# A six-layer transformer on one core: the next layer's projection weights split in halves, at places spread over two cycles

## The reference, cut to what matters

```python
def attn_layer(x, Wqkv, qs, ksc, Wo):
    qkv = x @ Wqkv
    ...
    q = l2norm(q) * qs
    k = l2norm(k) * ksc
    q = q * cos * scale + rotate_half(q) * sin * scale
    k = k * cos * inv + rotate_half(k) * sin * inv
    out = local_attention(q, k, v)
    return out @ Wo
for i in range(DEPTH):
    x = attn_layer(shift_tokens(x), Wqkv[i], q_scale[i], k_scale[i], Wo[i]) + x
    x = ffn_layer(shift_tokens(x), ln_g[i], ln_b[i], W1[i], b1[i], W2[i], b2[i]) + x
```

## Time and profile before

| | |
|---|---|
| median of 3 runs | 3810.37 us (3803.43 to 3812.31) |
| the profiled execution | 3809.82 us, its span 3808.0 us |
| TensorE, VectorE, ScalarE, GpSimd busy | 92%, 78%, 71%, 63% of the span |
| mean granted clock of TensorE | 0.978 |
| first projection of the layers | at 686.59 us of the span |

### The profile page before, as it was taken

One profiled execution on the slowest core, in us unless ns is written; L12 is line 12 of the kernel. 1 busy time (PEld: TensorE's weight loads), 2 busy tenths in 40 slices (PEclk: granted clock), 3 DMA queues, 4 the chain that ended last, 5 costly groups with the idle time before them and its releaser, 6 DMA issues. The chain is left out here.

```text
span 3808.0 us, 161553 instructions
## 1 busy us (share of the span) xinstructions
PE 3516.9 (92%) x67234; PEld 2893.7 (76%) x67234; DVE 2986.5 (78%) x4277; ACT 2686.3 (71%) x4153; POOL 2393.2 (63%) x2866
## 2 busy tenths in 40 slices
PE   5888888599999999999999999999999999999995
PEld 3555555378888888888888888888888888888874
DVE  3455554588888888888888888888888888888874
ACT  2444444377777778877778877888778887887772
POOL 1010000577777777777777777777777777777762
PEclk9999999799999999999999999999999999999997
DMA  1000000132222332222322223222232222322221
GB/s 54 4 3 3 6 3 3 41 89 69 67 70 63 74 90 70 70 66 73 90 66 66 66 72 90 66 66 66 72 89 67 67 71 63 75 71 68 67 66 56
DMA packets 161761, 228.28 MB, mean 60 GB/s; under 512 B 42259, under 2 KB 60633, under 8 KB 161497
## 3 DMA queue, kind: packets, MB, share of 16 engines
q1 hardware_dynamic: 161624, 226.85, 23.8%
HBM read 21.00 MB, written 4.19 MB: 7 GB/s over the span
## 5 line engine op out<-in xcount | busy, mean ns | idle before, releaser
L1109 POOL TENSOR_TENSOR by_cos<-by_cos,by_sin 128x1024 f32<-128x1024 f32 x384 | 921.3, 2399 | 49.2 <-DVE by_sin L1453 49.2
L1115 POOL TENSOR_TENSOR by_cos<-by_cos,norms 128x1024 f32<-128x1024 f32 x384 | 724.0, 1907 | 0.5 <-issue 0.3
L1451 DVE TENSOR_TENSOR by_cos<-proj,turns 128x1024 f32<-128x1024 f32 x384 | 470.0, 1224 | 216.6 <-ACT squares L1344 216.2
L1188 PE MATMUL proj<-qkv_hi,xs_hib 128*128 128x512 f32 x1152 | 523.9, 455 | 57.8 <-DVE by_sin L1453 42.2
L1344 ACT ACTIVATE squares<-proj 128x1024 f32<-128x1024 f32 x384 | 392.5, 1022 | 179.9 <-PE proj L1190 172.6
L1324 ACT ACTIVATE vb<-proj 128x1024 f32<-128x1024 f32 x192 | 195.4, 1017 | 422.7 <-PE proj L1190 401.1
L1453 DVE TENSOR_TENSOR by_sin<-proj,turns 128x1024 f32<-128x1024 f32 x384 | 466.1, 1214 | 0.0
L1457 DVE TENSOR_REDUCE sumsb<-squares 128x16 f32<-128x1024 f32 x384 | 464.0, 1208 | 1.5 <-DVE w_lo L1514 1.5
L1190 PE MATMUL proj<-qkv_hi,xs_lob 128*128 128x512 f32 x1152 | 459.2, 399 | 0.8 <-issue 0.8
L1189 PE MATMUL proj<-qkv_lo,xs_hib 128*128 128x512 f32 x1152 | 458.5, 398 | 0.0
L1197 PE MATMUL ring<-ident,by_cos 128*128 128x128 f32 x3072 | 404.4, 275 | 1.7 <-POOL by_cos L1115 0.8
(11 more groups left out here) (172 smaller groups left out, 8208.7 us busy)
## 6 DMA issues: line engine op xcount, KB each, us to landing
v_win<-vb SPq DMA_DIRECT2D x1152, 128.0 KB, 2.4
v_win<-vb SPq DMA_DIRECT2D x768, 64.0 KB, 2.0
in_qkv<-L_ffn_Wqkv SPq DMA_DIRECT2D x12, 768.0 KB
wo<-L_ffn_Wo SPq DMA_DIRECT2D x6, 512.0 KB, 4.0
x_tok<-L_attn_x SPq DMA_DIRECT2D x8, 256.0 KB, 4.7
residual<-x_tok SPq DMA_DIRECT2D x8, 256.0 KB, 2.0
o_x<-residual SPq DMA_DIRECT2D x1, 2048.0 KB, 7.9
out<-o_x SPq DMA_DIRECT2D x8, 256.0 KB, 2.3
```

Source lines behind the costliest of these rows:

```text
L1109: nc.gpsimd.tensor_tensor(both, both, by_sin[:, j, :], ALU.add).then_inc(e[f"{w_}_added"].sem, 1)
L1115: nc.gpsimd.tensor_tensor(heads, heads, inverse, ALU.mult).then_inc(e[f"{w_}_ready"].sem, 1)
L1188: nc.tensor.matmul(out, xs_hi[:, tile], qkv_hi[:, cols], start=True, stop=False)
L1451: nc.vector.tensor_tensor(of_heads(by_cos[:, t % 2, j, :]), heads, table(0), ALU.mult)
```

## The change

The three conversions of 1024 columns become six of 512, and each has a place of its own: a table, NEXT_WEIGHTS, says before which step of cycle 14 (-2) or 15 (-1) of a layer's end it is put. ScalarE rounds all six halves. VectorE subtracts four (lo_q0, lo_q1, lo_k1, lo_v0), GpSimd two (lo_k0, lo_v1). The four tables of turns are issued one by one. All semaphores are per half, and the readers wait for both halves of what they use: GpSimd's first XSd of the new layer for q, the first Cq for k and for the turns, the first Ck for v. At the start of the stage each engine does its own pieces first, in the order of the table.

```diff
+NEXT_WEIGHTS = {
+    "Act": {(-2, "MK:1"): "hi_q0", (-2, "EXP:0"): "hi_q1", (-2, "GEL"): "hi_k1", (-1, "EV:1"): "hi_k0",
+          (-1, "EXP:-1"): "hi_v0", (-1, "EX:-1"): "hi_v1"},
+    "DVE": {(-2, "AM"): "lo_q0", (-2, "Rk:3"): "turn_0 turn_1", (-2, "XN"): "lo_q1 turn_3",
+          (-1, "R:-2"): "turn_2", (-1, "Cq:2"): "lo_k1 lo_v0"},
+    "Pool": {(-1, "N:1"): "lo_k0", (-1, "Aq:2"): "lo_v1"},
+}
...
-    if at == -LEAD and engine in ("Act", "DVE"):
-        steps += [(("NQ", k), 0, "", 0) for k in range(3)]
+    if at == -LEAD:
+        steps += [((piece,), None, "", 0) for piece in " ".join(NEXT_WEIGHTS.get(engine, {}).values()).split()]
...
+        if end is None and at is not None and at >= STEPS - HALVES:
+            pieces = NEXT_WEIGHTS.get(engine, {}).get((at - STEPS, token), "").split()
+            steps += [((piece,), None, "", 1) for piece in pieces]
...
-        if tile == PER * STEPS - 1 and end is None:
-            for k, (act, dve) in enumerate((("Qq", "Rq"), ("Qk", "Rk"), ("EV", ""))):
-                if (engine, name) in (("Act", act), ("DVE", dve)):
-                    steps.append((("NQ", k), 0, "", 1))
-            if (engine, name) == ("DVE", "Rk"):
-                steps.append((("NT",), 0, "", 1))
-        if (engine, name) == ("DVE", "Cq") and tile == PER * STEPS and end is None:
-            steps.append((("NQ", 2), 0, "", 1))
...
+        def columns_of(x):
+
+            at = PART[x[0]] * INNER + int(x[1]) * (INNER // 2)
+            return slice(at, at + INNER // 2)
...
-                        pool.wait_ge(p_lo, new * 3 + 1)
+                        for half in "01":
+                            pool.wait_ge(p_lo["q" + half], new + 1)
...
+                elif kind[:3] == "lo_":
+                    x = kind[3:]
+                    cols = columns_of(x)
+                    pool.wait_ge(p_hi[x], new + 1)
+                    nc.gpsimd.tensor_tensor(qkv_lo[:, cols], in_qkv[:, cols], qkv_hi[:, cols].bitcast(F32),
+                                            ALU.subtract).then_inc(p_lo[x], 1)
...
+                elif kind[:3] == "hi_":
+                    x = kind[3:]
+                    act.wait_ge(loaded, all_loaded(new))
+                    if when[1] >= 0:
+                        event, tile = f"{x[0]}_proj", PER * STEPS - 1 - PER * p
+                        wait_tile(act, event, tile, when)
+                    cols = columns_of(x)
+                    copy(qkv_hi[:, cols], in_qkv[:, cols]).then_inc(p_hi[x], 1)
...
-                        dve.wait_ge(p_turns, new + 1)
+                        dve.wait_ge(p_turns, new * 4 + 4)
+                        for half in "01":
+                            dve.wait_ge(p_lo[("k" if w_ == "q" else "v") + half], new + 1)
...
+                elif kind[:5] == "turn_":
+                    n = int(kind[5:])
+                    scale = in_qs if n < 2 else in_ks
+                    nc.vector.scalar_tensor_tensor(
+                        out=turns[:, n, :, :], in0=tables[:, n, :, :], scalar=(QK_SCALE if n < 2 else 1.0) / ROOT_SCALE,
+                        in1=scale[:, :].unsqueeze(1).broadcast_to([P, TILES, DH]), op0=ALU.mult, op1=ALU.mult)\
+                        .then_inc(p_turns, 1)
```

More of the change, by code:

```diff
@@ L961, in layers_stage @@
         pool_ready = sem("pool_ready")
-        p_hi, p_lo, wo_loaded, p_w2 = sem("p_hi"), sem("p_lo"), sem("wo_loaded"), sem("p_w2")
+        wo_loaded, p_w2 = sem("wo_loaded"), sem("p_w2")
+        p_hi, p_lo = ({x: sem(f"p_{part}_{x}") for x in ("q0", "q1", "k0", "k1", "v0", "v1")} for part in ("hi", "lo"))
         p_w1_hi, p_col, p_used = sem("p_w1_hi"), sem("p_col"), sem("p_used")
@@ L1495, in step @@
                         .then_inc(e["x_mid"].sem, 1)
[L1496 to L1499, removed]
+                elif kind[:3] == "lo_":
+                    x = kind[3:]
+                    cols = columns_of(x)
+                    dve.wait_ge(p_hi[x], new + 1)
                     nc.vector.tensor_tensor(qkv_lo[:, cols], in_qkv[:, cols], qkv_hi[:, cols].bitcast(F32),
[L1501 to L1505, removed]
+                                            ALU.subtract).then_inc(p_lo[x], 1)
+                elif kind[:5] == "turn_":
[5 more added lines that the diff above has]
+                        .then_inc(p_turns, 1)
                 elif kind == "NF":
@@ L1520, in step @@
                     ffn(kind, b, when)
[L1522 to L1528, removed]
             def ffn(kind, b, when):
```

## The result

The changed kernel takes 3819.15 us (median of 8 runs, 3815.22 to 3824.95), the kernel before beside it 3807.82 (8 runs, 3803.43 to 3812.31): the ratio is 1.003, with a 95% interval of 1.0019 to 1.0041. The profiled execution took 3824.72 us, its span is 3822.9. One execution of the kernel before, among those beside e5_v_whole and b3_balanced, took 6572.57 us at a mean clock of 0.56 and enters no number here.

The account below looks back on a forecast made before the run. TensorE was busy 92% of the span, and a layer boundary cost 4.02 us more than two plain cycles. Boundaries +7.1, stage start +1.2 and clock +1 made +9.3 on 3809.8: 3819 us, range 3803 to 3828.

Parts of the forecast that it names:

- base: The profiled execution of the kernel before, 3809.8 us, 0.6 below the median of three runs, to which the terms were added.
- start term: At the stage's start, GpSimd's pieces ahead of its first XSd delay the first projection: +1.2 us once, bounds 0.3 and 2.5.
- clock term: TensorE stands still longer at each boundary, so the granted clock falls more: +1 us in all, bounds -1 and +4.
- Exclusion: VectorE operations reading two SBUF tensors and GpSimd ones wait out each other's whole instruction; whichever has waited goes next.
- The cost of a boundary: Cycles 14 and 15 at a layer's end: 5.4 us over two plain cycles instead of 4.0, five times +1.4 = +7.1.
- Splitting gained 0.7 us at XN: Cycle 14, VectorE: with the split, XN starts at t 29.43 against 30.17, winning 0.7 us there.
- the pair: Cycle 15, VectorE: lo_k1 waits for GpSimd's Ak:1 to 35.94, lo_v0 follows, Cq:2 starts at 37.14 instead of 35.08.
- Rival (a): Cycle 15: GpSimd's lo_v1 goes ahead of lo_v0, so lo_v0 and Cq wait 1.2 us more; 3825; chance 0.20.
- the 0.1 us: Cycle 15: lo_v1 is ready at about 36.64, lo_v0 starts at 36.54; Ak:1 that much later would let lo_v1 first.
- Rival (d): The clock drops at every boundary: the forecast + 4, 3823 us; chance 0.10.

Follow-up runs that it names:

- e5_v_whole: e4_halves_old_places with VectorE's two halves of v made one operation of 1024 columns again; 3814.17 us, ratio 1.0001 to the kernel before.
- b3_balanced: Changed kernel with Ak:1 ahead of N:1, VectorE's and GpSimd's pieces re-placed, all lo pieces on VectorE at the stage's start; 3802.65 us, 0.9970 of the kernel before.
- e1_read_psum: Changed kernel with VectorE's lo pieces at layer ends reading one PSUM input times zero instead of two SBUF tensors; 3804.43 us, ratio 0.9990 to the kernel before.
- e3_ak_first: Changed kernel with GpSimd's Ak:1 ahead of N:1 and turn_2 moved to cycle 14; 3811.98 us, ratio 1.0005 to the kernel before.
- e6_hi_v1_early: Changed kernel with ScalarE's hi_v1 moved directly behind hi_v0; 3829.58 us, ratio 1.0048 to the kernel before.
- the second profile: Changed kernel run and profiled again without any edit; 3822.29 us, ratio 1.0031 to the kernel before.
- e2_no_gpsimd_pieces: Changed kernel with GpSimd's two pieces at layer ends only raising their semaphores; 3812.26 us, ratio 1.0007 to the kernel before.
- e4_halves_old_places: Changed kernel with the six halves at the places of the old whole pieces, none on GpSimd; 3829.38 us, ratio 1.0045 to the kernel before.

## Why the prediction was right, point by point

The time was forecast at 3819.0 and came out at 3819.15. Part of that is luck: the kernel before had 3807.8 in the 8 runs beside the changed one, 2.6 below the three runs on which the forecast was put, and the sum was 2 us short (9.3 forecast, 11.3 measured): a base too high, a start term too large and a clock term too small nearly cancel. By its steps:

- **Exclusion, its length and, at the layers' ends, who goes next** held. lo_q0 at t 22.57, ending 24.74 (22.58 and 24.77 forecast); XN at 29.42 (29.43); Ak:1 at 33.68 (33.69); Cq:2 at 37.12 (37.14); Pk at 39.52 (39.55). e1_read_psum showed that the SBUF read is the cause, e3_ak_first that it is this one operation of GpSimd. That of two the one that has waited goes next, which the prediction gave as a rule, did not hold at the start of the stage in three of the kernels (b3_balanced above).
- **The cost of a boundary** was forecast at 67.2 and is 67.23 with the clock at 1.00. Splitting gained 0.7 us at XN, as said, and lost more at the pair.
- **Rival (a)** was put at 1.2 us a boundary above the forecast. e6_hi_v1_early, in which it happens, has Cq:2 1.07 us later than the changed kernel (t 38.19 against 37.12) and 1.4 us more in a boundary, where the clock fell in both: 69.7 in the mean against 68.3 at the nine such ends of the changed kernel. It needed the 0.1 us, and lo_v1 missed them: it was ready at 2719.30, and Cq:2 shows that lo_v0 had begun at about 2719.2 (2719.78 less the 0.60 of a half).
- **The start of the stage** was put at +1.2. At the first projection it is +0.9 (6.63 against 5.70), +1.3 in the second profile. By the first XC nothing of it is left: 105.5 and 107.0 against 106.75. The step that failed is that a later first projection makes a later stage; over the ten profiles the way from the first score to the first XC is 105.5 to 107.3 us, with no relation to where the first projection lies. That the delay comes from GpSimd's pieces is not shown either, as b3_balanced had +1.2 without them.
- **The clock** was put at +1, with bounds of -1 and +4. Worked out from the boundary pairs, the changed kernel lost 341.89 - 5 x 67.23 = 5.7 us to it, and 3.7 in the second profile, against 330.15 - 5 x 65.82 = 1.05 before: +2.7 to +4.7. This is the mis-sized term. I took one drop in five to stay the usual case, though the forecast itself had TensorE stand longer than before at every boundary. Rival (d), each boundary slowed, which had a chance of 0.10, is what happened, with the start term gone and so without its 3823. The step should have taken 1.05 x 5 from the earlier trace rows, as the rival did, or most of it.

So the sum by its terms is +7.1 (boundaries), 0 (start), +2.7 to +4.7 (clock): +9.8 to +11.8, and 11.3 was measured, 12.1 the second time.

**What stays open** is what decides the clock. The changed kernel and e6, with waits of 2.33 and 3.40 us ahead of Pk, lost it at 14 of 15 ends. The kernel before and e5_v_whole wait 2.02 and 2.09 us ahead of V and lost it at one in five each, as did e3_ak_first with 1.85 us there and e2_no_gpsimd_pieces with 1.51 ahead of V and 1.36 ahead of Pk. b3_balanced, with nothing above 0.95 us in these cycles, lost it at none. That far the length of the wait would do. But e1_read_psum has nothing above 1.28 us there and lost it at three ends, and e4_halves_old_places, with two waits at each (2.09 us ahead of V, 1.95 us for GpSimd's f_rstdb 13 us later), at all five. No run here separates the length of a wait from where it lies.

## What to carry to other kernels

Before a VectorE operation on two SBUF tensors is moved or split, lay it over GpSimd's timeline: its price is what is left of the GpSimd instruction that it meets, here up to 2.2 us on a half of 0.69, and a step of GpSimd moved by one place (and a turn with it) was worth 1.7 us a boundary where the split was worth 0.7. Splitting an operation also opens a place in its midst, into which an instruction that has waited can go; split only where nothing waits. And a wait of TensorE that a change makes longer should be charged with the matmuls behind it at half speed as well. Here a wait of 2.33 us had that price nine times in ten, 1.05 us in the mean; waits of 1.85 to 2.09 us had it at one end in five.

## What the runs showed of the hardware that was not expected

- Two halves back to back on VectorE let a waiting GpSimd instruction in between them: 3.48 us for a pair that is 1.21 as one piece. But not always: at the start of the stage, xs_lo on GpSimd had to sit out VectorE's next two pieces (1.85 us instead of 0.57).
- The same two turns took 0.74 us undisturbed and 1.28 or 1.84 (b3_balanced) beside GpSimd: the operation of two SBUF tensors and a scalar is excluded like the plain subtraction.
- An operand in PSUM lifts it: 1.29 us for two halves in the midst of GpSimd's 2.37.
- The clock fell to 0.51 behind a wait of 2.33 us at nine of ten layer ends of the changed kernel, and each drop cost 0.6 to 1.8 us.
- Code that no version touched, ahead of the stage, took between 680.9 and 690.4 us from profile to profile, nearly as much as the whole effect of this change.
